# A one-core graph network: in its first graph convolution, ScalarE makes every second set of one-hot columns for the dense table reads

## The reference, cut to what matters

```
deg = segment_sum(ones, col, n);  deg_out = segment_sum(ones, src, n)
norm = deg_inv_sqrt[row] * deg_inv_sqrt[col]
out = segment_sum(embedding_weight[row] * norm[:, None], col)      # first convolution
agg = segment_sum((features * norm_src[:, None])[src], dst)        # second convolution
```

## Time and profile before

| | |
|---|---|
| median of 3 runs | 5763.12 us (5759.78 to 5773.19) |
| profiled execution, its own time | 5738.98 us |
| its span in the trace | 5737.2 us |
| mean granted TensorE clock | 0.946 of full |
| first convolution in the trace | about 1027 to 1693 us |
| second convolution | about 1720 to 2290 us |

### The profile page before, as it was taken

How to read it: one execution, slowest core, us unless ns; L and a number is a source line. 1 busy time by engine, 2 the same in 40 slices (tenths; PEclk the granted TensorE clock), 3 DMA queues, 4 the chain that set the end, 5 groups by cost and what they waited for, 6 DMA issues and landing times.

```text
span 5737.2 us, 137892 instructions
## 1 busy us (share of the span) xinstructions
PE 4974.8 (87%) x47173; PEld 3432.1 (60%) x47173; DVE 3660.0 (64%) x7001; ACT 2116.4 (37%) x3942; POOL 3818.3 (67%) x3980
## 2 busy tenths in 40 slices
PE   4999999788878888599999986999999769999997
PEld 3777777788868888255555552555555535555554
DVE  7556555788877777465666674565666746655656
ACT  2222222555556665233333323333333233333331
POOL 5777776676637776677777716777777177777770
PEclk8999999899989999799999997999999889999998
DMA  5755555333323333344444423444444234444442
GB/s 143 190 162 169 168 168 148 85 93 87 85 73 100 101 101 83 81 128 128 121 124 123 127 66 85 126 127 124 125 123 123 62 95 125 128 124 123 122 122 62
DMA packets 694510, 667.19 MB, mean 116 GB/s; under 512 B 398707, under 2 KB 485242, under 8 KB 693818
## 3 DMA queue, kind: packets, MB, share of 16 engines
q1 hardware_dynamic: 558442, 489.21, 28.4%
q0 software_dynamic: 127424, 164.72, 13.8%
q10 hardware_dynamic: 7952, 4.46, 0.5%
HBM read 568.30 MB, written 89.59 MB: 115 GB/s over the span
## 4 chain that ended last, share of the span: by engine, by line
PE 57%; POOL 17%; issue 16%; DVE 7%; DMA 2%; DVEq 1%; ACT 1%; SPq 0%; ACTq 0%; POOLq 0%
PE ps L1071 18%; PE ps L916 13%; POOL rows L363 11%; PE ps L1010 8%; POOL rows L376 6%; PE ps L1031 4%; PE ps L931 3%; PE ps L1045 3%; PE ps L1021 2%; PE ps L996 2%; PE ps L990 1%; DMA rows<-table,idx 1%; DVE region L1778 1%; DVE acc L1803 1%; PE ps L943 1%
## 5 line engine op out<-in xcount | busy, mean ns | idle before, releaser
L376 POOL DMA_INDIRECT rows<-table,idx x2340 | 2252.0, 962 | 1082.9 <-issue 706.6
L1071 PE MATMUL ps<-region,hot 128*128 128x272 f32 x4992 | 1313.2, 407 | 172.8 <-DVE region L1756 84.3
L683 ACT ACTIVATE region<-ps 128x512 f32<-128x512 f32 x1248 | 677.7, 596 | 1678.6 <-PE ps L1010 1678.6
L1071 PEld LDWEIGHTS ps<-region,hot 128*128 128x128 f32 x4992 | 914.6, 193 | 467.6 <-issue 291.7
L1803 DVE TENSOR_TENSOR acc<-acc,ps 128x272 f32 x1248 | 544.3, 436 | 871.0 <-PE ps L1071 766.1
L916 PE MATMUL ps<-hot,region 128*128 128x192 bf16 (+1 forms) x9216 | 895.6, 256 | 50.7 <-DVE region L1630 28.2
L363 POOL DMA_INDIRECT rows<-table,idx x728 | 703.7, 967 | 245.1 <-issue 220.6
L916 PEld LDWEIGHTS ps<-hot,region 128*128 128x128 bf16 x9216 | 825.8, 102 | 60.6 <-DVE region L1630 31.4
L1778 DVE TENSOR_TENSOR region<-ps,region 128x1056 f32<-128x1056 f32 x582 | 724.6, 1251 | 44.8 <-issue 39.6
L1010 PE MATMUL ps<-xT,wcat 64*128 64x512 f32 x2496 | 713.9, 649 | 9.3 <-ACT region L683 9.1
L396 POOL DMA_INDIRECT rows<-table,idx x448 | 426.7, 952 | 197.0 <-issue 123.7
(11 more groups left out here) (302 smaller groups left out, 6583.4 us busy)
## 6 DMA issues: line engine op xcount, KB each, us to landing
hot<-hot_dram SPq DMA_DIRECT2D x624, 256.0 KB
turned<-turned_dram SPq DMA_DIRECT2D x624, 128.0 KB
rows<-table,idx POOLq DMA_INDIRECT x3516
hot_dram<-hot SPq DMA_DIRECT2D x104, 512.0 KB
region<-hot_dram SPq DMA_DIRECT2D x96, 512.0 KB
xwin<-table SPq DMA_DIRECT2D x1664, 24.0 KB
region<-r_dram SPq DMA_DIRECT2D x109, 256.0 KB, 5.4
region<-d_dram SPq DMA_DIRECT2D x104, 256.0 KB
```

Source lines behind the costliest of these rows:

```text
L376: pool.indirect_dma_start(rows[:, n % 2, j, :], None, table, bass.IndirectOffsetOnAxis(ap=idx[:, s:s + 1], axis=0)).then_inc(rows_in3[n % ...
L683: act.activation(rz[g % 2][:, 2 * t + side, :], ps[:, Z + side, :], ACT.Relu).then_inc(rz_made, 1)
L1071: mm = pe.matmul(ps[:, sum_bank(k, side, i), 0:PC + H], hot[:, b, 4 * side + 2 * i + j, :], px[b][:, 4 * side + 2 * i + j, :], start=(j == ...
```

## The change

In the first convolution ACT now makes the one-hot columns of the odd dense groups (1, 3, ..., 47), with the instructions that it uses in the second; DVE makes the even ones. ACT's sets stand between its degree groups: set 1 ahead of degree group 0, and set d (`made` in the code) ahead of the first degree group g with 48 g >= 104 (d - 1). Set 3 stands ahead of degree group 5, set 5 ahead of 9, set 7 ahead of 13. The semaphore counts follow.

```
         def stationary_there(d):
-            return (bt_made, FOLD * (d + 1)) if d < ND else (bt2_made, FOLD * (d - ND + 1))
+            if d < ND:
+                return (bt2_made if d % 2 else bt_made), FOLD * (d // 2 + 1)
+            return bt2_made, FOLD * (ND // 2 + d - ND + 1)
...
         def act_degree(act):
+            act_stationary(act, 1)
+            made = 3
             for g in range(G):
+                if made < ND and ND * g >= G * (made - 1):
+                    act_stationary(act, made)
+                    made += 2
                 b = g % 2
...
         def act_stationary(act, d):
-            b, at = d % 2, d - ND
+            b, at = d % 2, (d // 2 if d < ND else ND // 2 + d - ND)
             act.wait_ge(r_in[b], 16 * (d // 2 + 1))
-            act.wait_ge(dense_read, 4 * (d - 1))
+            if d >= 2:
+                act.wait_ge(dense_read, 4 * (d - 1))
...
-                    if pas == 1:
+                    if pas == 1 and d % 2 == 0:
                         v.tensor_scalar(bt[b][:, k, :], rline[b], lanes[:, k:k + 1], None, ALU.is_equal).then_inc(bt_made, 1)
```

## The result

The changed kernel takes 5857.28 us (median of 4 runs, 5852.52 to 5862.85), the kernel before 5761.45 us (4 runs, 5729.69 to 5773.19). The ratio of the runs is 1.0189, with a 95% interval of 1.0162 to 1.0216 (the two medians alone differ by 95.8 us, 1.7%): slower, with the forecast of 1.019 inside the interval. Whether it is more than 2% slower stays open. The traced execution of the change has a span of 5861.1 us, 123.9 more than that of before. Of these 117.4 lie in the first convolution, from its first to its last dense read: 658.2 us before (1027.29 to 1685.49), 775.6 now (1031.95 to 1807.52). 4.7 us come ahead of it and some 2 behind it, where nothing was changed.

The account below looks back on a forecast made before the run. PE and DVE were taken to share the path in the first convolution. Waits for ACT of 125 us, less 18 given back, plus 1 at the start, made +108 on 5763.12: 5871 us, range 5822 to 5908.

Parts of the forecast that it names:

- The loop: First convolution: PE's freeing read, ACT's set, the degree group queued behind, PE's next reads; waits of 125 us in 23 cycles.
- T to `degree(g)`: From the end of PE's read freeing the set's buffer to PE's start on the degree group behind the set: 11.8 us.
- What is given back: PE's stretch from that degree group to the next freeing read shortens: about 0.8 us a cycle, 18 us in all.
- one fall a cycle: After each wait PE's clock drops to its lower level once, making the next read 1.25 us longer.
- the bound of 18.1: PE's 21.0 us stretch behind the wait, at the second convolution's pace, would shrink to 18.1 us, 2.9 us less a cycle.
- The start: Set 1 delays degree group 0 by 4.6 us, mostly covered by a transfer wait of 3.50 us; 1.4 us left.
- The sum: Whole kernel: 125 - 18 + 1 = +108 us, giving 5871 us, a ratio of 1.019.
- more: Rival: the clock stays low longer than one short fall and DVE gives nothing back; +155 us, 5918 us; chance 0.08.
- Faster: Rival: DVE's 47.5 us leave the shared path and ACT's degree groups ahead cover the set; -45 us, 5718; chance 0.04.
- its deciding point: The faster rival decides where 11.8 us after the freeing read comes before PE's request; longest time here 9.3 us.
- The pace of the second convolution in full: Rival of smaller loss: PE regains that pace entirely; +59 us, 5822; within the forecast's range, beyond it chance 0.05.

Follow-up runs that it names:

- e1: Changed kernel with each of ACT's sets two degree groups later in its list: 5695.15 us against 5742.99 for the kernel before, ratio 0.9907; first convolution 608.4 us.
- e4: Changed kernel with the Relu left out of ACT's sets in the first convolution: that stage 665.4 us against 775.6 for the changed kernel.
- e6: Kernel before, with ACT only waiting for the changed kernel's freeing reads and making no set: first convolution 650.2 us against 658.2 before.
- e9: Changed kernel with each of ACT's sets three degree groups later in its list: first convolution 726.6 us against 775.6 for the changed kernel.
- e10: Changed kernel with 70 or 140 zero matmuls on PE ahead of the 23 degree groups behind a set: first convolution 731.8 us.
- e11: The changed kernel traced once more, nothing altered, to see the variation: first convolution 776.2 us against 775.6.

## Why the prediction was right

*The loop.* T to `degree(g)` was to be 11.8 us; it is 11.75 in 22 of 23 cycles and 12.02 in one. The waits were to be 125 us in 23 cycles; they are 132.8 with the 4.5 us of the first degree group, so 128 in the 23. They come to a little more since PE reaches `degree(g)` sooner than before, 6.2 us after T in the mean in place of 6.37. A set takes 8.07 us here too (1417.77 to 1422.13 + 3.71). That it is the order and not ACT's load is shown from four sides: the same load in another place gives 608 us (e1), a shorter set gives 42.6 us of waits (e4), the wait with no set 3.8 us (e6), and one group too late brings waits at another place (e9). One sign was misjudged: ACT was to wait 3 to 5 us a cycle for PE's read, and waits 8.7 (201 us in 23 cycles). Its 23.7 us of work had been set against the old cycle of 27.4 us and not against the new one of 32.4; the sum did not use it.

*What is given back.* Here a size was off. I took 0.8 us a cycle net, 18 us. By the cycles of the trace it is 21.0 before against 32.40 - 11.76 = 20.6 us from `degree(g)` to the next T, 0.4 us, some 9 in all. The parts were larger on both sides: PE's other waits fell by 90.5 - (188.8 - 132.8) = 34.5 us, and the reads' excess grew by 16.4, as falls went from 26 to 35 and, after the long waits, a read took up to 4.16 us where I had used 3.47. I had priced one fall a cycle, 23 x 1.25 = 29 us, and the reads' excess is 55.9 us in 35 falls. That the falls hold this back is seen in e10: with 8 of them the stretch from `degree(g)` to the next T is 18.5 us, close to the bound of 18.1.

*The start.* 1.4 us were said; from the first read to T of set 3 it is 32.4 us against 30.0, so 2.4 (1.2 in e11). The wait for the transfer was covered as said, but behind the wait of 4.5 us the second read took 4.16 us, where before it took 2.22.

*The sum.* +108 us were said; it is +117.4 in the traced stage, +109 by the ratio of the runs and +96 by their medians. That the ratio meets the forecast to a tenth of a percent is luck: in the stage the forecast is 9 us short, nearly all of it in what is given back (by the cycles +124 for T to `degree(g)`, 9 back, 2 at the start), and the runs of before spread over 43 us. *The rivals:* "more" was right that the clock stays low for longer than one short fall a cycle (184 us of the stage, against 89 before), but it had nothing given back and another 1.25 us a cycle lost, and 0.4 us a cycle came back. "Faster" was right in that its mechanism exists: with the groups ahead of the set, as e1 has them, DVE's relief gives 49.8 us where I had put 45, but the change as made never reaches its deciding point. Its sum was right for a wrong reason: two thirds of e1's gain are the clock (reads' excess 39.5 to 6.7 us) and only 15.8 are waits. "The pace of the second convolution in full" did not come; the falls stayed, and only e10, with few of them, comes near it.

## What to carry to other kernels

Before giving work to an engine with much idle time, look at when it is idle, and write down its list: what stands behind the new instruction, who waits for that, and whether the new instruction itself waits for that same engine's progress. If so it is a loop, and its length against the time at which the result is asked for tells the waits before anything is run; what the clock adds or takes has to be priced by itself. Put what others wait for ahead of the instruction that must wait: here two degree groups ahead turned a loss of 1.9% into a gain of 0.9%, one more and the stage was 68 us longer than before again.

## What the runs showed of the hardware

The clock was worth more than I had thought. From before to e1, waits of PE fell by 16 us but its reads became 33 us shorter, at 3 falls in place of 26. And matmuls of zeros in PE's waits, 121 us of them, made the stage 44 us shorter in place of longer (776.2 to 731.8 us, clock 0.88 to 0.97). In the changed kernel the clock record shows 184 us of the stage at 1.2 GHz, against 89 us before; 50 of the 95 us of difference lie inside PE's waits for ACT, where a low clock costs nothing: the reads' excess grew by 16 us only.

The stages ahead of the first convolution, which no kernel here changes, ended between 1023 and 1048 us from run to run. That is why the stage's own length and not the span was compared in the single runs.
